# SyncE loads to number 47, GpSimd reports to number 39, stores three groups and loads from 48 on

## What is computed

```python
def reference(x, itok_B_0_63, L0_cond_W, L0_cond_b):
    selected_W = W[cat_ids]
    selected_b = b[cat_ids]
    out = jnp.einsum('bsd,bdh->bsh', x, selected_W) + selected_b[:, None, :]
    return x + out
```

## Time and profile before

| | us |
|---|---|
| median of 3 runs (lowest, highest) | 100.14 (100.07, 100.21) |
| the profiled execution, whole | 100.16 |
| its span, first to last instruction | 98.4 |
| PE busy | 88.4 |
| DVE busy | 57.4 |
| ACT busy | 56.4 |
| POOL busy | 33.6 |

### The profile page before, as it was taken

The page is one execution under the profiler, slowest core; times in us unless marked ns, Lnnn a source line. Parts: engine busy times, 40 slices in busy tenths (PEclk is TensorE's granted clock), DMA queues, the critical chain, the costliest instruction groups (busy, mean ns, idle before and its releaser), DMA issues.

```text
span 98.4 us, 3042 instructions
## 1 busy us (share of the span) xinstructions
PE 88.4 (90%) x788; PEld 58.6 (60%) x788; DVE 57.4 (58%) x139; ACT 56.4 (57%) x98; POOL 33.6 (34%) x63
## 2 busy tenths in 40 slices
PE   0229499999999999999999999999999999999980
PEld 0126257666666667676757575857676767676740
DVE  2736430688787693747466665666555646463840
ACT  4102426965834756766676764867585858585500
POOL 5100000000000029999986566785323480000000
PEclk9999999999999999999999999999999999999999
DMA  1999999999999998899999999999998799996363
GB/s 18 340 308 343 353 350 349 348 351 350 348 353 351 349 348 242 258 333 315 395 361 393 358 406 358 400 388 388 376 386 290 208 330 320 347 336 205 110 210 110
DMA packets 19891, 31.19 MB, mean 317 GB/s; under 512 B 1505, under 2 KB 15906, under 8 KB 19874
## 3 DMA queue, kind: packets, MB, share of 16 engines
q0 software_dynamic: 4640, 16.26, 46.8%
q1 hardware_dynamic: 13330, 12.91, 40.9%
q10 hardware_dynamic: 1904, 1.84, 5.9%
HBM read 25.23 MB, written 8.39 MB: 342 GB/s over the span
## 4 chain that ended last, share of the span: by engine, by line
PE 85%; DMA 7%; DVE 2%; issue 1%; SPq 1%; ACT 1%; POOLq 0%; DVEq 0%
PE mm_ps L584 56%; PE xt_ps L492 17%; PE mm_ps L570 8%; DMA w_all<-in_L_cond_W 6%; PE mm_ps L498 2%; PE xt_ps L584 2%; DMA cats_i<-in_itok_B 1%; SPq L169 1%; ACT w_slot L327 1%; DVE rows L461 0%; DVE same_ahead L409 0%; PE mm_ps L503 0%; DVE has_place L421 0%; PE mm_ps L510 0%; DVE cats L401 0%
## 5 line engine op out<-in xcount | busy, mean ns | idle before, releaser
L584 PE MATMUL mm_ps<-w_slot,xT 128*64 128x256 f32 x496 | 58.0, 386 | 0.6 <-ACT w_slot L327 0.6
L327 ACT COPY w_slot<-w_all 128x512 f32 x64 | 39.0, 619 | 26.1 <-PE mm_ps L584 9.7
L584 PEld LDWEIGHTS mm_ps<-w_slot,xT 128*64 128x64 f32 x496 | 34.7, 139 | 18.0 <-issue 1.3
L461 DVE TENSOR_TENSOR rows<-mm_ps,rows 128x512 f32<-128x512 f32 (+1 forms) x32 | 21.6, 675 | 28.2 <-PE mm_ps L584 27.8
L183 POOL DMA_DIRECT2D w_all<-in_L_cond_W x32 | 16.4, 515 | 40.2 <-DMA w_all<-in_L_cond_W 33.6
L327 DVE COPY w_slot<-w_all 128x512 f32 x64 | 26.7, 454 | 3.6 <-POOLq L199 3.0
L339 ACT COPY xT<-xt_ps 128x512 f32<-128x512 f32 x32 | 17.3, 584 | 8.9 <-PE xt_ps L492 8.9
L492 PE MATMUL xt_ps<-ident,rows 128*128 128x128 f32 x128 | 19.2, 298 | 0.0
L492 PEld LDWEIGHTS xt_ps<-ident,rows 128*128 128x128 f32 x128 | 15.1, 151 | 6.8 <-issue 6.8
L570 PE MATMUL mm_ps<-bias_parts,is_sample 96*64 96x256 bf16 x124 | 10.3, 288 | 0.7 <-ACT xT L339 0.7
L214 POOL DMA_DIRECT2D out<-rows x11 | 8.8, 800 | 1.1 <-issue 0.6
(11 more groups left out here) (46 smaller groups left out, 12.8 us busy)
## 6 DMA issues: line engine op xcount, KB each, us to landing
w_all<-in_L_cond_W POOLq DMA_DIRECT2D x32, 256.0 KB
w_all<-in_L_cond_W SPq DMA_DIRECT2D x28, 256.0 KB, 6.1
out<-rows POOLq DMA_DIRECT2D x11, 512.0 KB, 8.1
rows<-in_x POOLq DMA_DIRECT2D x9, 512.0 KB, 7.2
rows<-in_x SPq DMA_DIRECT2D x6, 512.0 KB, 6.7
out<-rows SPq DMA_DIRECT2D x8, 256.0 KB, 4.0
w_all<-in_L_cond_W ACTq DMA_DIRECT2D x4, 256.0 KB, 5.8
rows<-in_x ACTq DMA_DIRECT2D x1, 512.0 KB, 3.9
```

Of the source, the lines that this page charges most:

```text
L327: copy(w_slot[:, PAIR * p + half, :, :].rearrange("p k h -> p (k h)"), w_all[:, bass.ds(c, 1), :, :].rearrange("p c k h -> p (c k h)")).th ...
L461: V.tensor_tensor(to, sums, to, ALU.add).then_inc(sums_added, 1)
L584: last = T.matmul(to[HALF * half:HALF * (half + 1), :], xT[:, slot, k, j, :], w_slot[:, j, k, :], start=False, stop=(k == K - 1), skip_gro ...
```

## The change

SP's list goes to load 47 (`SYNC_LOADS` 48), with the conditional loads 40 to 47 and with rows 6 to 11 between them; rows 10 and 11 keep their wait for the stores of groups 0 and 1. GpSimd reports loads 0 to 39 (`POOL_REPORTS` is `SYNC_LOADS` less 8) and then stores groups 0, 1 and 2 in a row (`STORED_AHEAD`). It reads two list words and the number of loads, waits for 45 reports (`REPORTED_FIRST`), and makes the loads from 48 on, rows 12 to 15, and the stores of groups 3 to 10 at places of their own. SP reports loads 40 to 63, after its last load.

```diff
--- before.py
+++ after.py
@@ -19,10 +19,10 @@
 WEIGHT_SLOTS = 8
 LOADS_IN_FLIGHT = 8
 FIRST_LOADS = 8
-SYNC_LOADS = 32
+SYNC_LOADS = 48
 POOL_REPORTS = SYNC_LOADS - LOADS_IN_FLIGHT
-REPORTED_FIRST = 29
-WORDS_AHEAD = 12
+REPORTED_FIRST = 45
+WORDS_AHEAD = 14
 CERTAIN_LOADS = 40
 WORD = 4
 BITS = 6
@@ -39,7 +39,8 @@
 
 
 X_AFTER_LOAD = {3: 13, 4: 19, 5: 25, 6: 31, 7: 33, 8: 37, 9: 40, 10: 43, 11: 46, 12: 48, 13: 51, 14: 55, 15: 60}
-STORE_AFTER_LOAD = {0: 37, 1: 40, 2: 43, 3: 46, 4: 48, 5: 51, 6: 59}
+STORED_AHEAD = 3
+STORE_AFTER_LOAD = {3: 48, 4: 49, 5: 51, 6: 59}
 POOL_GROUPS = 11
 
 
@@ -64,7 +65,9 @@
     assert WEIGHT_SLOTS == GROUP and PAIRS_IN_GROUP == WORD and C % LOADS_IN_FLIGHT == 0
     assert FIRST_LOADS % WORD == 0
     assert all(at + 1 >= min(C, GROUP * (g + 1) + QUAD - 1) for g, at in STORE_AFTER_LOAD.items())
-    assert all(X_AFTER_LOAD[g + X_SLOTS] >= STORE_AFTER_LOAD[g] for g in range(GROUPS - X_SLOTS))
+    assert all(X_AFTER_LOAD[g + X_SLOTS] >= STORE_AFTER_LOAD[g] for g in range(STORED_AHEAD, GROUPS - X_SLOTS))
+
+    assert X_AFTER_LOAD[X_SLOTS] + 1 >= max(POOL_REPORTS, GROUP * STORED_AHEAD + QUAD - 1)
 
 
     x_groups = x.rearrange("(g p h) s d -> g (h s) p d", p=PAIRS_IN_GROUP, h=PAIR)
@@ -238,7 +241,13 @@
                 if n >= FIRST_LOADS + LOADS_IN_FLIGHT:
 
                     sp.wait_ge(w_loads_done, n - LOADS_IN_FLIGHT + 1)
-                load_weights(sp, n, part(word, n % WORD))
+                if n == CERTAIN_LOADS:
+                    loads = words_read(mybir.EngineType.SP, load_words[0:1, LIST_WORDS:LIST_WORDS + 1], C)[0]
+                if n >= CERTAIN_LOADS:
+
+                    load_weights(sp, n, part(word, n % WORD), cond=loads > n)
+                else:
+                    load_weights(sp, n, part(word, n % WORD))
                 rows_after(sp, n)
 
             sp.wait_ge(w_loads_done, POOL_REPORTS)
@@ -287,7 +296,10 @@
 
             for n in range(POOL_REPORTS):
                 report(pool, n)
+            for g in range(STORED_AHEAD):
+                store_sums(g)
             words = [list_word(w) for w in range(SYNC_LOADS // WORD, WORDS_AHEAD)]
+            loads = words_read(mybir.EngineType.Pool, load_words[0:1, LIST_WORDS:LIST_WORDS + 1], C)[0]
 
             pool.wait_ge(w_loads_done, REPORTED_FIRST)
             for n in range(SYNC_LOADS, C):
@@ -295,21 +307,16 @@
 
                     words.append(list_word(n // WORD + 1))
                 word = words[(n - SYNC_LOADS) // WORD]
-                if n == CERTAIN_LOADS:
-                    loads = words_read(mybir.EngineType.Pool, load_words[0:1, LIST_WORDS:LIST_WORDS + 1], C)[0]
                 if n >= SYNC_LOADS + LOADS_IN_FLIGHT:
 
                     pool.wait_ge(w_loads_done, n - LOADS_IN_FLIGHT + 1)
-                if n >= CERTAIN_LOADS:
-
-                    load_weights(pool, n, part(word, n % WORD), cond=loads > n)
-                else:
-                    load_weights(pool, n, part(word, n % WORD))
+
+                load_weights(pool, n, part(word, n % WORD), cond=loads > n)
                 rows_after(pool, n)
                 for g, after in STORE_AFTER_LOAD.items():
                     if after == n:
                         store_sums(g)
-            for g in range(len(STORE_AFTER_LOAD), POOL_GROUPS):
+            for g in range(STORED_AHEAD + len(STORE_AFTER_LOAD), POOL_GROUPS):
                 store_sums(g)
 
         def slots_of(engine, g, half):
```

## The result

The changed kernel takes 107.75 us (median), the kernel before beside it 100.17: a ratio of 1.072, 95% interval 1.061 to 1.083. The forecast was 104.2, range 102.5 to 107.0: slower, as forecast, but by almost twice as much, and outside the range. The profiled execution took 107.66 us, its span is 106.0 against 98.4.

What follows compares the result with a forecast made beforehand. TensorE, full from 12.4 to 95.7 us, was taken as the bound. The five steps put its restart in group 7 at 59.5 instead of 55.5, a 4.0 us stall: 100.16 + 4.0 = 104.2 us, range 102.5 to 107.0.

Steps and rivals of the forecast that it cites:

- the filled dip: DMA rate of 249 GB/s from 36.9 to 41.8 us; filling it brings 1.4 us of transfer earlier, worth 0.
- The clock: TensorE's clock falls to 1.2 GHz in the 4 us stall, another 2.6 us lost: 106.8 us; chance 0.15.
- Step 1: Load 39 lands at 48.1 us: 3.67 MB at 350 GB/s, 10.5 us behind 37.7.
- Step 2: GpSimd issues store 0 0.3 us after load 39 has landed, at 48.4 us.
- Step 3: Store 0 takes 5.3 us from issue to landing, to 53.7 us; bounds 3.9 and 6.9.
- the second rival: Store 0 lands in 4.6 us, or even 3.9: 103.5 us, down to 102.8; chance 0.13.
- Step 4: SP's rest of the list, rows 10 to load 47, takes 4.9 us, to 58.6 us.
- Step 5: Report of load 40 and release 0.15, copy 0.62, then 0.14 us: PE starts at 59.5 us.
- the store has its way: Store 0, hardly slowed by SP's loads, lands in 4.6 or 3.9 us: 103.5, down to 102.8; chance 0.13.
- No stall: SP comes through its list by 54.7 us, PE stays full: 100.16 us, not slower; chance 0.05.
- a second stall: Rows 10 or the loads behind them late as well, a further 1 to 3 us: 105.5 to 107; chance 0.07.
- The end of the kernel: The 2.7 us from 95.7 us to the end of the span, which the change was said not to touch.

Runs made afterwards that it cites:

- the run with both edits: Changed kernel with its three stores made behind the report of load 31 and loads 40 to 43 reported before SyncE waits for store 0: 102.21 us, ratio 1.021.

## Why the prediction was wrong

The chain was right, each link of it seen in the profile: what bounds the kernel, that the filled dip is worth nothing, that load 40's report stands behind the list, that PE waits once, in group 7, at the last pair, and that nothing behind it is late. The run with the held report and the one with the report moved show it from both sides. It was wrong in the size, in two terms of its sum: the sum took the stall for the whole loss, with nothing for the clock behind it, and the stall itself came out too short.

1. **The clock was a rival (0.15) and should have been part of the sum.** It is 2.0 us of the 3.6 that were missing (7.6 less 4.0). The forecast asked only whether a stall of 4.0 us might be long enough; the measured one was 5.6. By the length of the wait in the profiled execution, the clock fell in all of four runs each at 4.8 and 4.9 us, in three of four at 3.6, in none at 2.0. The trace of before had the price right in kind (2.6 us in the first 7.1) and said that PE, idle for most of the first 12 us, came out of it at the lower level (the run with six added products was busy there and came out at the same level, so that idleness alone is not the reason there). The argument against, that PE had been full for 40 us, is refuted: what PE did before the stall does not carry it through. The Trainium skill (TensorE: Matmul & The Clock Gate, Part 1) puts an idle PE at the lower level, 1.2 GHz; the trace agrees, with a granted clock of 0.50 from 59 to 60 us, while it waited, and of 0.53 from 61.07 to 65.5.
2. **The stall was 5.6 us instead of 4.0.** By its steps:
   - Step 1, load 39 at 48.1: it was reported at 49.1, + 1.0. The engines did move 349 GB/s as assumed; but a load counts when the last of its 16 parts has landed, and the parts had drifted apart. For load 31 they landed from 36.2 to 37.7, for load 39 from 46.7 to 49.1, where eleven had landed by 47.1 and the other five came from 48.1 on. The first part came 10.5 us behind that of load 31, as the sum has it. Why five fall back is open.
   - Step 2, 0.3 us to the store: 0.7, + 0.4.
   - Step 3, store 0 in 5.3 us: 4.8, - 0.5. The bounds (3.9 and 6.9) held, and the second rival's value was near.
   - Step 4, 4.9 us for the rest of the list: 5.5, + 0.6; from the tenth rows to load 44 it took 2.03 us instead of 1.41, because the word read took 0.94 us instead of 0.28. In the run with the stores behind report 37 it took 0.26.
   - Step 5, 0.9 us: 0.95.

   The sum of these is + 1.6, PE at 61.07 for 59.5; each is small, and all but one have the same sign. The range had room for one of them or for the clock, not for both: 102.5 to 106.0 for the stall and 106.8 for the clock at a stall of 4.0 were never added. A stall at its upper bound with the measured price of the clock would have been 106.0 + 2.0 = 108.0.

The rival that the store has its way was argued from turns by packet: by these store 0 would hardly feel SyncE's loads. 4.8, 5.6, 6.8 and 7.4 us with more and more of SyncE's transfers under way speak against that as a price, so here the measurement decides. That store 0 took only 4.8 us in the changed kernel, near the rival's 4.6, has another reason: SyncE stood before the tenth rows and sent nothing more. Where it went on, the same store took 7.2. "No stall" was rightly given 0.05, and "a second stall" did not come. The end of the kernel was called untouched; in the changed kernel it was, but the trace of the run with both edits suggests that a list that ends later can cost there.

## What to carry to other kernels

When an engine signals for others behind its own work list, ask of each entry that is added to the list who is waiting for the signal behind it: here a single report, late by 10 us, cost 7.6, and reporting four loads earlier gave nearly all of it back. When a full TensorE gets a stall as long as these (3.6 us and up here; nothing was measured between 2.0 and 3.6), put the clock into the sum, not beside it. And when transfers are made earlier in one place, look at where the last ones now end.

## What the runs showed of the hardware

- The clock fell in or just behind waits of 3.6 (three of four runs), 4.8, 4.9 and 5.3 us and not at one of 2.0, in a PE that had been full for over 35 us. At 3.6 and 4.9 it fell only when PE was back at work. Getting back cost 1.6 to 2.2 us in the traces, less than the 2.6 of the start. 20 useless products in the wait kept it up.
- The records of the granted clock begin with its first rise, 15.4 to 18.0 us into the span; the 1.00 that the profile shows ahead of it is no measurement, and the products there took twice their later time.
- With products of 256 columns in the waits at the start the clock was up by 9.2 us in one trace and at 9.9 in the other; six of 128 columns, with PE as busy (7.7 of the 8.0 us from 4.4 on, in both), left it down until about 16. Which property of a product counts is open.
- The same 512 KB store took 4.8 to 7.4 us from issue to landing, longer with more of another engine's transfers under way (1.6 to 2.4 MB).
- One list word read by SyncE took 0.26, 0.42 and 0.94 us in three runs, at the same place of the list. What delayed it is open.
